# Attention 2: expert results mixed over four units, and the next step's projections one unit later

## The reference

```python
h = h + expert_ffn(layernorm(h))            # per token: h += sum over its 4 experts of share * result
x = layernorm(h)
q, k, v = 8 heads of 24 from x @ w_qkv.T
origin = softmax(q k' * scale) v            # 8 heads
head_x = 0
for i in (0, 1):                            # two groups of 96 columns, in turn
    cur = x[:, group i] + head_x
    q2, k2, v2 = cur @ w_gi.T
    head_x = softmax(q2 k2' * scale) v2
    out_i = head_x + origin[:, group i]
h = h + concat(out_0, out_1) @ w_proj.T + b_proj
```

## Time and profile before

| | |
|---|---|
| median of 3 runs | 981.94 us (981.36 to 992.75) |
| profiled execution | 989.29 us, span 987.6 us, mean granted TensorE clock 0.842 |
| busy over the span | TensorE 82%, VectorE 50%, ScalarE 31%, POOL 37% |
| attention 2 | from about 430 to about 634 us of the span |
| unit 0's transpose of steps 0, 1, 2, 3 | 448.96, 488.59, 537.71, 581.22 us |

### The profile page before, as it was taken

How to read it: one execution, slowest core, us unless ns; L and a number is a source line. 1 busy time by engine, 2 the same in 40 slices (tenths; PEclk the granted TensorE clock), 3 DMA queues, 4 the chain that set the end, 5 groups by cost and what they waited for, 6 DMA issues and landing times.

```text
span 987.6 us, 14813 instructions
## 1 busy us (share of the span) xinstructions
PE 809.7 (82%) x4860; PEld 580.6 (59%) x4860; DVE 495.7 (50%) x1223; ACT 306.8 (31%) x571; POOL 365.1 (37%) x233
## 2 busy tenths in 40 slices
PE   7988872189899999988979788779799899878572
PEld 4665662056667777756767574554646656656351
DVE  4355654524634445748675864363724643533210
ACT  1121421023333333323423337244342253342200
POOL 3015888786810387668786100010200010000000
PEclk9687765579999999987969898959689689989795
DMA  8821113334542344452111000000000000000000
GB/s 234 261 79 47 35 29 72 74 75 117 121 122 82 89 116 111 107 154 62 32 31 27 1 1 1 1 1 1 2 0 2 14 0 0 12 3 1 14 0 15
DMA packets 81395, 52.96 MB, mean 54 GB/s; under 512 B 42942, under 2 KB 76719, under 8 KB 80305
## 3 DMA queue, kind: packets, MB, share of 16 engines
q1 hardware_dynamic: 25026, 28.25, 9.9%
q0 software_dynamic: 40960, 11.98, 6.7%
q10 hardware_dynamic: 15344, 11.87, 4.2%
HBM read 29.53 MB, written 21.69 MB: 52 GB/s over the span
## 4 chain that ended last, share of the span: by engine, by line
PE 64%; DVE 12%; POOL 11%; issue 6%; ACT 3%; DMA 1%; SPq 0%; DVEq 0%; ACTq 0%; POOLq 0%
PE ex_up L1138 6%; PE ex_up L1139 6%; POOL xs_scratch L209 5%; POOL work L220 4%; PE ps L2267 3%; PE ps L2198 3%; PE ex_yp L1161 3%; PE ex_yp L1162 3%; PE ps L1347 2%; PE ps L1354 2%; PE ps L1352 2%; PE ps L1628 2%; PE ps L2207 2%; PE ps L1353 2%; PE a_ps L389 1%
## 5 line engine op out<-in xcount | busy, mean ns | idle before, releaser
L220 POOL DMA_INDIRECT work<-ys_scratch,place x64 | 153.2, 2393 | 88.9 <-DMA ys_scratch<-ex_yb 58.3
L209 POOL DMA_INDIRECT xs_scratch<-e_t,e_routed x64 | 153.1, 2392 | 43.8 <-issue 30.2
L1239 DVE TENSOR_SCALAR ex_bb<-ex_up 128x384 f32<-128x384 f32 x44 | 24.6, 558 | 119.9 <-PE ex_up L1139 88.5
L1138 PE MATMUL ex_up<-e_wa,ex_x 128*128 x176 | 76.7, 518 | 8.1 <-issue 5.3
L1139 PE MATMUL ex_up<-e_wb,e_ex_x 65*128 x176 | 74.7, 506 | 0.0
L2477 POOL TENSOR_TENSOR H<-H,f_hh 113x768 f32 (+1 forms) x4 | 7.2, 1807 | 144.7 <-DVE f_hh L2620 144.7
L2455 POOL TENSOR_SCALAR f_veps<-f_mv 113x4 f32<-113x4 f32 x10 | 1.9, 195 | 147.8 <-DVE f_mv L2517 147.8
L2403 ACT ACTIVATE f_pT<-ps 113x452 f32<-113x452 f32 x48 | 26.2, 547 | 82.0 <-PE ps L2207 81.8
L1139 PEld LDWEIGHTS ex_up<-e_wb,e_ex_x 65*128 65x128 f32 x176 | 35.1, 200 | 25.4 <-issue 3.4
L1196 ACT ACTIVATE ex_sg<-ex_up 128x384 f32<-128x384 f32 x44 | 21.6, 492 | 86.4 <-PE ex_up L1139 79.4
L1138 PEld LDWEIGHTS ex_up<-e_wa,ex_x 128*128 128x128 f32 x176 | 31.2, 196 | 26.3 <-issue 13.7
(11 more groups left out here) (372 smaller groups left out, 1954.4 us busy)
## 6 DMA issues: line engine op xcount, KB each, us to landing
ex_xb<-xs_scratch SPq DMA_DIRECT2D x88, 96.0 KB
ys_scratch<-ex_yb ACTq DMA_DIRECT2D x44, 192.0 KB
e_wa<-in_wa SPq DMA_DIRECT2D x4, 1152.0 KB
xs_scratch<-e_zeros SPq DMA_DIRECT2D x46, 96.0 KB
e_wb<-in_wb SPq DMA_DIRECT2D x4, 576.0 KB
e_wa<-in_patches SPq DMA_DIRECT2D x4, 432.0 KB, 9.3
xs_scratch<-e_zeros ACTq DMA_DIRECT2D x16, 96.0 KB
out<-H SPq DMA_DIRECT2D x4, 339.0 KB
```

The costliest lines, as they stand in the source:

```text
L209: nc.gpsimd.indirect_dma_start(out=dram.xs, out_offset=bass.IndirectOffsetOnAxis(ap=S.pos[:, j, k:k + 1], axis=0), in_=S.t[:, j, :], in_of ...
L220: nc.gpsimd.indirect_dma_start(out=S.yk[:, it % 2, j, k, :], out_offset=None, in_=dram.ys[it // X.steps], in_offset=bass.IndirectOffsetOnA ...
L1138: mm(o, x1[:, p % 3, t], S.wa[:, bass.ds(w, 2 * I)], start=True, stop=False)
```

## The change

On VectorE the four experts' mixings of the next step stand at units 0, 1, 3 and 4, one expert each, instead of two each at units 0 and 1. `h_stat` moves from unit 2 to unit 4, `norm` from 4 to 5, and X2's copy from 5 to 6. On TensorE `pre_x` moves from unit 5 to 6, `pre_group` from 6 to 7, the first `pre_qk` from 7 to 8 and the second from 8 to 9. The scores of the next step's first unit now follow the first projection within unit 8, and those of its second and third come at unit 9 behind that unit's transpose, with the second projection behind them. ScalarE's copies and VectorE's K copies move along; VectorE's first K copy stands ahead of the softmax input at unit 8. GV0 is copied by ScalarE instead of VectorE. POOL's and SP's queues are not edited.

```diff
--- before.py
+++ after.py
@@ -1547,7 +1547,7 @@
 
 
         X1, X2, GQ0, GK0, Q0, K0, Q1, K1, V0, V1, GV0 = range(11)
-        proj = Tiles(nc, ctx, "a1_proj", bank[4:6], ["act", "dve", "act", "act", "act", "dve", "act", "dve", "dve", "act", "dve"])
+        proj = Tiles(nc, ctx, "a1_proj", bank[4:6], ["act", "dve", "act", "act", "act", "dve", "act", "dve", "dve", "act", "act"])
 
         HX0, GQ1, GK1, GV1, HX1, O1, O2, HH0, HH1 = range(9)
         group = Tiles(nc, ctx, "a1_group", bank[6:8], ["dve", "act", "act", "dve", "act", "dve", "dve", "dve", "dve"])
@@ -1757,10 +1757,6 @@
                         scores(it, n + 2, n + 3)
                     if n == 5:
                         scores(it, n + 2)
-                    if n == 8 and not last:
-                        scores(it + 1, 0)
-                    if n == 9 and not last:
-                        scores(it + 1, 1, 2)
                     if n == 6:
                         back(it, 0)
                     turn(it, n)
@@ -1772,13 +1768,15 @@
                         second_group(it)
                     if n == 4:
                         second_values(it)
-                    if n == 5 and not last:
+                    if n == 6 and not last:
                         pre_x(it + 1)
-                    if n == 6 and not last:
+                    if n == 7 and not last:
                         pre_group(it + 1)
-                    if n == 7 and not last:
+                    if n == 8 and not last:
                         pre_qk(it + 1, 0)
-                    if n == 8 and not last:
+                        scores(it + 1, 0)
+                    if n == 9 and not last:
+                        scores(it + 1, 1, 2)
                         pre_qk(it + 1, 1)
                     if n == 2 and last:
                         pe.wait_ge(*proj.copied(it, V1))
@@ -1830,6 +1828,10 @@
                 cp(v[:, 2:4, :, 0:HD], proj.bank(V1)[0:N, 0:2 * D].rearrange("p (g h d) -> p g h d", g=2, h=HEADS), ACT.Copy
                    ).then_inc(proj.out(V1), 1)
 
+            def pre_gv(it):
+                act.wait_ge(*done(proj.filled, it, GV0))
+                cp(gv[:], images(proj.bank(GV0)[0:N, 0:G * GD]), ACT.Copy).then_inc(proj.out(GV0), 1)
+
             def exp(it, n):
                 act.wait_ge(*units.copied(it, n))
                 pp = p[:, n % SLOTS, :, :]
@@ -1850,6 +1852,7 @@
                     exp(0, n)
                 evac(0, proj, Q1, q[:, 1, :], 128)
                 pre_v(0)
+                pre_gv(0)
 
             def body(it, first, last):
                 for n in range(NU):
@@ -1889,6 +1892,7 @@
                 outputs(it, 1)
                 if not last:
                     pre_v(it + 1)
+                    pre_gv(it + 1)
                 else:
                     nxt.pre_v(0)
 
@@ -1940,9 +1944,6 @@
             def pre_v(it):
                 evac(it, proj, V0, v[:, 0:2, :, 0:HD], proj.bank(V0)[0:N, 0:2 * D].rearrange("p (g h d) -> p g h d", g=2, h=HEADS))
 
-            def pre_gv(it):
-                evac(it, proj, GV0, gv[:], images(proj.bank(GV0)[0:N, 0:G * GD]))
-
 
             def softmax_in(it, n):
                 sc = images(units.bank(n)[0:N, 0:GN])
@@ -2007,36 +2008,34 @@
                 normalise(0, 0)
                 pre_k(0, 1)
                 pre_v(0)
-                pre_gv(0)
 
             def body(it, first, last):
                 for n in range(NU):
                     if n == 2:
                         first_result(it)
+                    if n == 8 and not last:
+                        pre_k(it + 1, 0)
                     if n + AHEAD < NU or not last:
                         softmax_in(*unit(it, n + AHEAD))
                     if n == 0 and not first:
                         late_o(it - 1)
                     if n == 1 and not first:
                         late_h(it - 1)
-                    if n in (0, 1) and not last:
-                        mixed(nc, dve, S, it + 1, 2 * n)
-                        mixed(nc, dve, S, it + 1, 2 * n + 1)
-                    if n == 2 and not last:
+                    if n in (0, 1, 3, 4) and not last:
+                        mixed(nc, dve, S, it + 1, n - n // 2 + n // 4)
+                    if n == 4 and not last:
                         dve.wait_ge(S.mixed, G * TOPK * (it + 2))
                         h_stat(nc, dve, S, it + 1)
-                    if n == 4 and not last:
+                    if n == 5 and not last:
                         norm(it + 1)
                     if n == 4:
                         evac(it, group, GV1, gv[:], images(group.bank(GV1)[0:N, 0:G * GD]))
-                    if n == 5 and not last:
+                    if n == 6 and not last:
                         pre_x(it + 1)
                     if n == 6:
                         normalise(it, 1)
                         divide(it, 0)
-                    if n == 7 and not last:
-                        pre_k(it + 1, 0)
-                    if n == 8 and not last:
+                    if n == 9 and not last:
                         pre_k(it + 1, 1)
                     if n == 9 and not last:
                         normalise(it + 1, 0)
@@ -2062,8 +2061,6 @@
                 else:
                     nxt.pre_v(0)
                 divide(it, 1)
-                if not last:
-                    pre_gv(it + 1)
 
             def tail(it):
                 late_o(it)
```

## The result

The changed kernel takes 998.02 us (median of 20 runs, 988.23 to 1008.98) beside 986.28 us for the kernel before in the same session (20 runs). The ratio is 1.0146, 95% interval 1.0117 to 1.0174: **slower by 14.3 us** (11.5 to 17.1). The ratio leaves out slow runs, those over 1.5% above the fastest of the same kernel, and one low run before (971.16) makes these many there; by the medians of all 20 runs the difference is 11.7 us. The direction is clear, the size is 12 to 14 us, and at 1.5% it lies within the 2% to which the forecast gave 0.95. The forecast was 990, range 980 to 998; the median lies at the range's very top and just outside. The profiled execution took 999.01 us, span 997.2, mean granted clock 0.842.

The account below looks back on a forecast made before the run. Fronts were taken as bound by VectorE, tails by TensorE, with POOL handing on step 0's later statistics. +8.8 by step 2's end and -0.4 in step 3 gave +8.4 on 981.9: 990 us, range 980 to 998.

Parts of the forecast that it names:

- POOL's gap before the tenth gather: A 4.02 us gap among POOL's sixteen gathers before step 1's root, assumed to keep its length.
- rival 1: POOL's gap closes, so step 1's root comes at 513.4, not 517.4; +2.4 to +4.4, 984 to 986 us; chance 0.16.
- Rival 3: Tails hide the new TensorE waits, staying at 20 to 21 us, and fronts shrink; 972 to 974 us; chance 0.10.
- tail: From scores of units 8 and 9 to the next step's unit 0 transpose; step 0 forecast 24.3 us against 19.6.
- POOL bounds step 1: Step 1's norm waits for POOL's root at 517.4, though VectorE could be ready earlier; step 1 ends at 541.8 before clock.
- front: From unit 0's transpose to the start of scores of units 8 and 9; step 2 forecast 20.7 us against 23.5.
- 4.4 us of slack: In step 1, root at 517.4 minus VectorE ready at 513.0; would absorb further loss in step 0.
- the step *Clock: Low TensorE clock adds 2 us (0 to 4) in step 1's tail; 2.5 us gaps in other tails cost nothing.
- rival 4: The clock holds throughout, neither fronts nor tails falling to half rate; +6.4, 988 us; chance 0.15.
- number 2: The low clock comes into every tail, 2 more in step 1 and 3 in step 2; +15, 997 us; chance 0.15.
- the rule for short gaps: The skill page's rule: a long idle gap puts TensorE back to half rate, shorter ones do not.
- the 2.54 row: A 2.54 us TensorE gap before scores at 592.06, still 1.05 long, taken as showing no low clock behind it.

Follow-up runs that it names:

- r2_change: The changed kernel, unedited, profiled in another execution; steps 0 to 2 took 147.0 us, step 3 took 51.25.
- r3_before: The kernel before, unedited, profiled in another execution; step 1's tail took 19.94 us, step 3 took 50.27.
- e8_fill_after: The changed kernel with nine small unused matmuls on TensorE before the scores of units 5 and 6 in steps 0 to 2; ratio to the kernel before 1.0144.
- e1: The changed kernel with mixing as before (two experts each at units 0 and 1) and statistics at unit 2; ratio to the kernel before 1.0122.
- e3: The kernel before with mixing spread over units 0, 1, 3 and 4, statistics and norm at unit 4; ratio to the kernel before 1.0104.
- e4: The changed kernel with POOL's root of step 1 behind five gathers of step 3, not eight; ratio to the kernel before 1.0215.
- e6: The changed kernel with ScalarE copying GQ0, GK0 and Q0 ahead of the exp they stood behind; ratio to the kernel before 1.0163.
- e7: The same as e6, and VectorE normalises the second group (unit 7) ahead of unit 8's softmax input; ratio to the kernel before 1.0111.
- e14: The same as e7, with POOL's root of step 1 behind six gathers of step 3; ratio to the kernel before 1.0143.
- e13_best: Kernel before; GV0, GV1 on ScalarE, root behind six gathers, unit 4's input before first group result, steps 1 and 2 mixing at units 1 to 3; 979.69 us.
- e2_gv_only: The kernel before with GV0 copied by ScalarE instead of VectorE; ratio to the kernel before 0.9997.
- e11_root6: The kernel before with GV0 copied by ScalarE and POOL's root of step 1 behind six gathers of step 3, not eight; ratio 1.0011.
- r1_change: The changed kernel, unedited, profiled in one more execution; steps 0 to 2 took 140.4 us, step 3 took 56.95.

## Why the prediction failed, point by point

**Held.** Most waits came where they were told. Set back by the later start of the phase (452.26 less 448.96, 3.3), the statistics of step 0 end at 467.8 (forecast 467.3), POOL's gap before the tenth gather is there again (3.88), and the second root ends at 517.1 (forecast 517.4):

```profile
500.48 2.37 POOL L220 DMA_INDIRECT work<-ys_scratch,place  x1 [3.88 <-issue]
...
519.37 1.05 POOL L251 TENSOR_TENSOR n_rstd<-n_veps,mhalf 113x4 f32<-113x4 f32 x1
```

So rival 1 is out. The stands are at unit 7's transpose (2.12, 2.12, 2.53; forecast 2.5), ahead of the next scores (1.25 in each step; forecast 1.35), ahead of the first q projection (0 to 0.44; forecast 0.65), and 2.54 to 2.59 ahead of the scores of units 5 and 6 (forecast 2.8 in step 2). Rival 3 is out too: no tail is under 23.5.

Steps 0 to 2 took 140.4 us (forecast 141.0), and this nearness is partly luck. Against the execution that the forecast started from they grew by 8.2 us, 7.1 of it busy time of TensorE and 1.1 stands; the forecast's 8.8 was 2 of clock and 6.8 of everything else.

**Held in one execution only: POOL bounds step 1.** In r2_change the front is 19.72 (forecast 19.5) and VectorE stands for the root; in the first execution VectorE reaches the norm 0.66 us after the root has ended, and there is no stand. The first line is r2_change, the second the changed kernel's first profile, both VectorE:

```profile
519.60 2.63 DVE L259 TENSOR_SCALAR n_x<-H,n_mv,n_rstd 113x192 f32<-113x192 f32 x4 [3.20 <-POOL n_rstd L251]
```
```profile
521.08 2.67 DVE L259 TENSOR_SCALAR n_x<-H,n_mv,n_rstd 113x192 f32<-113x192 f32 x4
```

The 4.4 us of slack were indeed there to "swallow what step 0 might lose further", and did: step 0 came out 3.96 us longer than forecast (48.50 against 44.54) and step 1 5.4 shorter (44.94 against 50.3).

**Failed: the step *Clock*.** It gave 2 us (0 to 4), in step 1's tail alone, priced the gaps of 2.5 us in the other tails at nothing, and left step 3 without any; rival 4 gave even less. The kernel loses more, in places that change with the execution: step 0's tail at 0.87 and step 3 at 0.85, or else step 1's tail at 0.73 (step 1 then takes 51.5, forecast 50.3) and step 2's at 0.82 (28.8, forecast 25.5). The sum for the phase was 141.0 + 52.9 = 193.9; three executions gave 197.7 on average, 3.8 on top of the 2. These 3.8 are what is left over, not a price of the clock: by the means of three, busy time of TensorE grew by 11.8 us for the same matmuls and the stands by 2.7, where the forecast's 8.4 was 2 and 6.4. Part of the longer busy time only fills stands that a front had anyway.

The forecast let a gap of 2.5 us go free because the scores behind one at 592.06 in the earlier trace rows were at full clock. The projection behind those scores tells against it, in the same trace (in r3_before it takes 1.68, at 590.16):

```profile
593.52 2.45 PE L1607 MATMUL ps<-a_cur,w1g 96*96 96x452 f32 x4
```

The same gap at 510.94 and 555.88 of the changed kernel is followed by projections of 3.2 us. So the 2.54 row is no row of a harmless gap, and the forecast was wrong to count it as agreeing with the rule for short gaps. Of the rivals, number 2 (+15, 997) named this cause and has about the size, though not quite the place: the tails were not all low, and step 3, which it left out, was.

**Failed: the base.** The difference was taken from one execution of the kernel before, and it was the longest of three: low clock in step 1's tail (0.85, 22.5 us) and in step 3 (0.94, 53.3 us). The mean of three phases is 183.2, 2.4 below it. (Its front of step 0 was the shortest of the three, 20.0 against 23.1.) So the 14.5 between the phases is 8.4 that was forecast, 3.8 left over and 2.4 of base; the terms are formed so that they add up, and prove nothing. Besides, the forecast was added to a median of 3 runs, 981.9; the median of 20 is 986.3. That shift of 4.3 carries over half of the 7.7 us between 990.3 and 998.0, and the difference of medians (11.7, forecast 8.4) the rest.

**What stays open.** No run held the clock by itself, so that it carries the larger part of the loss is read from the busy times of three executions each and is not shown by an experiment; e8_fill_after was meant to and didn't, and the timed runs put less on it. Nor is it known what puts the low clock where it is in an execution. e1, e3, e4, e6, e7 and e14 each took away a named stand, or one part of the change, and all stay at 1.010 to 1.022: no single stand is the cause.

## What to carry to other kernels

Ask first where the moved work lands. Norm and projections one unit later, with the mixing left alone (e1_late_only), cost 1.2% by themselves: they put waits into the tails, where TensorE was busy 93 to 97% of the time. Work that is moved off a front's busy engine must also come out ahead of everything that depends on it: here the statistics are the head of a chain through POOL and sixteen gathers, and spreading the mixing put them behind two softmax inputs. Before a sum is made against one profile, ask what that execution's own clock added to it, stretch by stretch; compare busy time of the same matmuls, then stands. e13_best is a better order of the same work: copies on the engine that is least busy, the root just ahead of where it is wanted, the order of the tails kept. The first two alone (e2_gv_only, e11_root6) gained nothing that can be told.

## What the runs showed of the hardware

- Executions repeat in patterns: r1_change and the first profile agree to 0.02 us in each stretch, while r2_change differs by up to 8.3 us in one stretch; sums differ by 0.9. Over 64 timed runs of the kernel before, time falls by 7.1 us for each 0.01 of mean granted clock.
- The granted clock fell behind the scores at 503.94 in e8_fill_after (projection 3.22 us, 1.68 at full clock) although TensorE had stood only 0.85 us ahead of them.
- The last of a row of indirect gathers has its data 5.65 us (e4) and 5.73 us (e14) after its issue ended, 2.36 us each to issue and 0.30 between. The forecast had "over 5 us" of room for it and no row.
- Four normalising instructions on VectorE take 2.1 to 2.7 us while POOL issues gathers (2.09 at 463.52 of the kernel before, 2.67 at 521.08 of the changed one) and 1.24 when it doesn't (567.09 of the changed kernel).
